# Attention core of a macaron block: probabilities times values in 512-query pieces instead of 256-query chunks

## The reference

```python
x = x + 0.5 * ffn(layernorm(x), ...)          # 8 experts of low rank, top 2
x = x + attn(layernorm(x), wq, wk, wv, wo)    # 16 heads of 128
x = x + 0.5 * ffn(layernorm(x), ...)

# attn
q = rope(einsum('bsd,dnh->bsnh', x, wq)) / sqrt(128)
k = rope(einsum('bsd,dnh->bsnh', x, wk))
v = einsum('bsd,dnh->bsnh', x, wv)
logits = where(causal, einsum('bqnh,bknh->bnqk', q, k), -1e30)
probs = softmax(logits)
attn = einsum('bnqk,bknh->bqnh', probs, v)
return einsum('bqnh,nhd->bqd', attn, wo)
```

## Time and profile before

| what | value |
|---|---|
| median of 3 runs | 1491.52 us (1490.91 to 1491.75) |
| profiled execution, device time | 1489.62 us |
| its span, first to last instruction | 1487.5 us |
| PE matmul / weight load | 1419.2 us (95%) / 1261.8 us (85%) |
| DVE / ACT / POOL busy | 1072.3 / 912.1 / 782.8 us |
| granted TensorE clock, mean | 0.992 |

### The profile page before, as it was taken

One profiled execution on the slowest core, in us unless ns is written; L12 is line 12 of the kernel. 1 busy time (PEld: TensorE's weight loads), 2 busy tenths in 40 slices (PEclk: granted clock), 3 DMA queues, 4 the chain that ended last, 5 costly groups with the idle time before them and its releaser, 6 DMA issues.

```text
span 1487.5 us, 25689 instructions
## 1 busy us (share of the span) xinstructions
PE 1419.2 (95%) x8932; PEld 1261.8 (85%) x8932; DVE 1072.3 (72%) x2395; ACT 912.1 (61%) x1890; POOL 782.8 (53%) x694
## 2 busy tenths in 40 slices
PE   6999999699999999999999999999999988999998
PEld 4778888589998999899989998999899877878886
DVE  7776876777767777777677767776777777775665
ACT  4544444577767767777777667776776654544433
POOL 4655454355555555555555555555555533755443
PEclk9999999899999999999999999999999999999999
DMA  4000001000000000000000000000000020000000
GB/s 167 1 1 1 1 1 50 22 7 23 1 8 15 8 8 8 15 9 8 15 2 8 22 1 8 22 1 8 8 1 1 1 111 1 1 15 1 15 15 15
DMA packets 11422, 23.40 MB, mean 16 GB/s; under 512 B 928, under 2 KB 5024, under 8 KB 11168
## 3 DMA queue, kind: packets, MB, share of 16 engines
q1 hardware_dynamic: 11296, 21.78, 4.4%
HBM read 19.68 MB, written 2.10 MB: 15 GB/s over the span
## 4 chain that ended last, share of the span: by engine, by line
PE 83%; DVE 9%; POOL 3%; issue 3%; ACT 1%; DMA 0%; DVEq 0%; POOLq 0%; ACTq 0%
PE ps L1439 24%; PE ps L1441 24%; PE ps L1440 24%; PE ps L1824 9%; DVE ps L1379 2%; DVE pT_l L327 1%; POOL um_l L327 1%; PE ps L1452 1%; POOL hid_l L327 1%; DVE hid L1079 1%; DVE mixed L1089 1%; POOL w_l L327 0%; POOL mixed_l L327 0%; DVE stats L934 0%; DVE xn L953 0%
## 5 line engine op out<-in xcount | busy, mean ns | idle before, releaser
L624 POOL TENSOR_SCALAR probs<-probs,inv_sum 128x128 f32<-128x128 f32 (+7 forms) x256 | 211.8, 828 | 387.1 <-DVE inv_sum L1314 387.1
L1379 DVE CUSTOM_DVE_ANT_0 ps<-ps,causal 128x128 f32<-128x128 f32 (+7 forms) x256 | 194.7, 761 | 211.0 <-PE ps L1441 209.2
L879 ACT ACTIVATE probs<-ps,neg_max 128x128 f32<-128x128 f32 (+7 forms) x256 | 189.1, 739 | 81.8 <-DVE neg_max L1379 81.8
L327 POOL TENSOR_TENSOR hid_l<-hid,hid_h 128x512 fp32r<-128x512 f32 x80 | 109.5, 1369 | 188.1 <-ACT hid_h L724 188.1
L327 DVE TENSOR_TENSOR pT_l<-ps,pT_h 128x512 fp32r<-128x512 f32 (+3 forms) x384 | 200.4, 549 | 2.8 <-ACT pT_h L858 2.6
L858 ACT ACTIVATE pT_h<-ps 128x512 fp32r<-128x512 f32 (+3 forms) x384 | 174.4, 491 | 34.6 <-PE ps L1824 32.1
L613 POOL TENSOR_TENSOR rot_sin<-swapped,rope 128x512 f32<-128x512 f32 x128 | 165.4, 1292 | 54.7 <-ACT swapped L835 54.7
L1824 PE MATMUL ps<-ident,probs 128*128 128x128 f32 x1152 | 170.9, 275 | 23.1 <-DVE pT_l L327 20.0
L1441 PE MATMUL ps<-pT_h,v_l 128*128 128x256 f32 (+1 forms) x640 | 179.0, 280 | 0.0
L1440 PE MATMUL ps<-pT_l,v_h 128*128 128x256 f32 (+1 forms) x640 | 178.9, 279 | 0.0
L1439 PE MATMUL ps<-pT_h,v_h 128*128 128x256 f32 (+1 forms) x640 | 178.1, 278 | 0.1
(11 more groups left out here) (190 smaller groups left out, 4076.4 us busy)
## 6 DMA issues: line engine op xcount, KB each, us to landing
w_raw<-attn_w SPq DMA_DIRECT2D x32, 256.0 KB, 2.6
w_in<-ffn_w SPq DMA_DIRECT2D x12, 576.0 KB, 8.3
x_sb<-x_in SPq DMA_DIRECT2D x4, 512.0 KB, 5.5
out<-x_sb SPq DMA_DIRECT2D x3, 512.0 KB, 3.2
rope<-rope_w SPq DMA_DIRECT2D x1, 1024.0 KB, 7.7
w_in<-ffn_w SPq DMA_DIRECT2D x2, 264.0 KB, 3.8
expand_raw<-expand_w SPq DMA_DIRECT2D x2, 256.0 KB, 4.8
out<-x_sb SPq DMA_DIRECT2D x2, 256.0 KB, 2.1
```

What stands on the lines that cost most here:

```text
L327: return eng.tensor_tensor(dst, src, high.bitcast(F32), ALU.subtract)
L624: pool.tensor_scalar(probs[s % 4][:, 0:n], probs[s % 4][:, 0:n], inv_sum[:, s % 4:s % 4 + 1], 1.0, ALU.mult, ALU.mult).then_inc(probs_read ...
L879: act.activation(probs[t % 4][:, 0:a * n].rearrange("p (a n) -> p a n", a=a), view, ACT.Exp, bias=neg_max[:, t % 4:t % 4 + 1], scale=-1.0, ...
L1379: dve.tensor_tensor_reduce(out=view, in0=view, in1=causal[:, SEQ - a * n:].rearrange("p (a n) -> p a n", a=a), scale=-SCALE, scalar=HUGE, ...
```

## The change

The diff does the following.

- PV works on 512 queries, half a unit. There are two halves c = 0, 1. Half 0 has key tiles 0 to 3, with 512, 384, 256 and 128 columns. Half 1 has key tiles 0 to 3 with 512 columns each, and key tiles 4 to 7 with 512, 384, 256 and 128. In all, 12 triples per unit in place of 20.
- PV of a unit lies wholly in the steps of the next unit, by the table `PV_AT`: half 0 in step 0, and half 1 in pieces in steps 3, 4, 5 and 6. Step 2 has none.
- The transposed probabilities lie in two tiles: `before` (key tiles 0 to 3 against the queries of half 1) and `own` (the two triangles). `tile_groups` gives the same sizes as before, in another order of key tiles.
- PV results are evicted 512 columns at a time, in steps 1 and 7.
- There is one copy of q. ACT's write of its high part waits until the scores that read the old one are done.
- Values: quarters 0 and 1 of a batch in steps 5 and 7 of the odd unit, quarters 2 and 3 in steps 1 and 7 of the even unit. Output projections: steps 3 and 5 of the even unit and 1 and 3 of the odd one. In the last pair other tables hold, and some layer-norm work of the second feed-forward block moves by one or two steps.
- The order within a step is scores, side work, output projection, PV, transpositions.

```diff
-T_LAG, PV_LAG, OUT_LAG = 2, 5, 8
+T_LAG = 2
-PAIR_SPLITS_AT = {"o": 7, "v": 17, "k": 21, "q": 23}
-DRAIN_STEPS = OUT_LAG + 1
+PAIR_SPLITS_AT = {"o": 13, "v": 25, "k": 21, "q": 23}
+DRAIN_STEPS = 8
+PV_AT = {0: (0, [0, 1, 2, 3]), 3: (1, [0]), 4: (1, [1, 2]), 5: (1, [3, 4]), 6: (1, [5, 6, 7])}
+O_AT = {1: 0, 7: 1}
+DRAIN_PV_AT = {32: (0, [0, 1, 2, 3]), 35: (1, [0, 1, 2, 3, 4, 5, 6, 7])}
+DRAIN_O_AT = {33: 0, 36: 1}
+Y_AT = {3: 0, 5: 1, 9: 2, 11: 3}
+LAST_Y_AT = [{19: 0, 21: 1, 24: 2, 25: 3}, {34: 0, 35: 1, 37: 2, 38: 3}]
-STATS_AT = [20, 21, 23, 24, 35, 37, 39]
-AGGREGATE_AT = [21, 24, 37]
-NORM_AT = [(23, 24), (25, 26), (38, 39)]
+STATS_AT = [20, 22, 25, 26, 35, 36, 39]
+AGGREGATE_AT = [22, 26, 37]
+NORM_AT = [(23, 24), (27, 27), (38, 39)]
 def tile_groups(i):
-    first = 1 - i % 2
-    out = []
-    while first <= i + 1 - i % 2:
-        n = min(4, i + 2 - i % 2 - first)
-        out.append((first, n))
-        first += n
-    return out
+    return [(False, i + 1)] if i < 4 else [(True, 4), (False, i - 3)]
...
+                if i == 1:
+                    q_h = sbuf(st, "q_h", [P, SEQ], F32R)
+                    q_l = sbuf(st, "q_l", [P, SEQ], F32R)
+                    before_l = sbuf(st, "before_l", [P, 4, 512], F32R)
+                k_h.append(sbuf(st, f"k_h{i}", [P, SEQ], F32R))
+                k_l.append(sbuf(st, f"k_l{i}", [P, SEQ], F32R))
...
+        def weighed_row(c, row):
+            if c == 1 and row < 4:
+                return slice(0, 512), (before_h[:, row], before_l[:, row])
+            d = row % 4
+            if c == 0:
+                cols, at = slice(P * d, 512), slice(4 * P * d, 4 * P * d + P * (4 - d))
+            else:
+                cols, at = slice(0, P * (4 - d)), slice(P * (16 - 3 * d), P * (20 - 4 * d))
+            return cols, (own_h[:, at], own_l[:, at])
...
+            if u % 2 == 0 and i in (1, 7):
+                k = 2 + i // 7
+                return "v", u // 2, 4 * (2 * p + u // 2) + k, k
+            if u % 2 == 1 and i in (5, 7) and not (u == UNITS - 1 and last):
+                k = i // 7
                 return "v", (u // 2 + 1) % 2, 4 * (2 * p + u // 2 + 1) + k, k
...
             def rope_high(index, u, k):
                 act.wait_ge(proj_rot, index + 1)
+                if k % 2 == 1 and index >= 4:
+                    act.wait_ge(scores_done, SEQ_TILES * (index // 4 - 1) + 4 * (k // 2) + 4)
...
+            def weigh(q, u, c, rows, first_unit):
+                final = 3 + 4 * c
+                index = 8 * q + 2 * u + c
+                if rows[0] == 0:
+                    need(pe, o_ready, index)
+                if c == 0:
+                    pe.wait_ge(pT_ready, groups_through(q, SEQ_TILES * u + 3))
+                elif rows[0] == 0:
+                    pe.wait_ge(pT_ready, groups_through(q, SEQ_TILES * u + 7) - 1)
+                if c == 1 and 4 in rows:
+                    pe.wait_ge(pT_ready, groups_through(q, SEQ_TILES * u + 7))
...
+                for row in rows:
+                    w = tuple(v[:, b, row, HD * head:HD * head + HD] for v in (v_h, v_l))
+                    cols, probabilities = weighed_row(c, row)
+                    ins = product(ps[:, PV_BANK, cols], w, probabilities, row == 0, row == final, skip=True)
...
-                    chunk = chunk_of_step(p, t, PV_LAG, first)
-                    if chunk:
-                        weigh(*chunk, first and chunk[0] == 0)
-                    y = out_of_step(p, t, OUT_LAG, first)
+                    y = y_of_step(p, t, first, last)
                     if y:
-                        project_out(*y, misc_bank(t))
+                        project_out(*y, y_bank(p, t, last))
+                    work = weigh_of_step(p, t, first)
+                    if work:
+                        weigh(*work, first and t < 2 * SEQ_TILES)
```

More of the change, by code:

```diff
@@ L416, in side_work @@
                 return "v", 0, k, k
-            if u % 2 == 1:
-                if u == UNITS - 1 and last:
-                    return None
+            if u % 2 == 0 and i in (1, 7):
[3 more added lines that the diff above has]
+                k = i // 7
                 return "v", (u // 2 + 1) % 2, 4 * (2 * p + u // 2 + 1) + k, k
@@ L438, in tile_of_step, with unit_before, weigh_of_step, o_of_step @@
             return None if (first and t < lag) or t - lag >= STEPS else (q, s)
-        def chunk_of_step(p, t, lag, first):
-            tile = tile_of_step(p, t, lag, first)
-            if not tile or tile[1] % 2 == 0:
-                return None
-            q, s = tile
-            u, i = unit_of(s)
-            return u, i // 2, 16 * q + 4 * u + i // 2, q, s
-        def out_of_step(p, t, lag, first):
-            chunk = chunk_of_step(p, t, lag, first)
-            if not chunk or chunk[0] % 2 == 0:
-                return None
-            u, c, _, q, _ = chunk
-            return u // 2, c, 4 * (2 * q + u // 2) + c, q
+        def unit_before(p, t, first):
+            if first and t < SEQ_TILES:
+                return None
+            return (p, t // SEQ_TILES - 1) if t >= SEQ_TILES else (p - 1, UNITS - 1)
+        def weigh_of_step(p, t, first):
+            unit = unit_before(p, t, first)
+            work = PV_AT.get(t % SEQ_TILES) if t < STEPS else DRAIN_PV_AT.get(t)
+            return unit + work if unit and work else None
+        def o_of_step(p, t, first):
+            unit = unit_before(p, t, first)
+            c = O_AT.get(t % SEQ_TILES) if t < STEPS else DRAIN_O_AT.get(t)
+            return unit + (c, 8 * unit[0] + 2 * unit[1] + c) if unit and c is not None else None
+        def o_place(u, c, high):
+            if u % 2 == 0:
+                return (oA_h if high else oA_l)[:, 512 * c:512 * c + 512]
+            return (oB_h if high else oB_l)[:]
+        def y_of_step(p, t, first, last):
+            if last:
+                for b in range(BATCH):
+                    if t in LAST_Y_AT[b]:
+                        return p, b, LAST_Y_AT[b][t], 4 * (2 * p + b) + LAST_Y_AT[b][t]
+            if t >= 2 * SEQ_TILES and t - 2 * SEQ_TILES in Y_AT and not last:
+                q, b, c = p, 0, Y_AT[t - 2 * SEQ_TILES]
+            elif t < 2 * SEQ_TILES and t in Y_AT and not first:
+                q, b, c = p - 1, 1, Y_AT[t]
+            else:
+                return None
+            return q, b, c, 4 * (2 * q + b) + c
+        def y_bank(p, t, last):
+            return MISC_BANKS[-1] if last and t >= STEPS - SEQ_TILES else misc_bank(t)
         def score_view(slot, i):
@@ L863, in attention @@
                         rope_high(turn[2], turn[1], turn[3])
-                    chunk = chunk_of_step(p, t, PV_LAG + 1, first)
-                    if chunk:
-                        u, c, index, _, _ = chunk
-                        dst = oA_h[:, 256 * c:256 * c + 256] if u % 2 == 0 else oB_h[:, c % 2]
+                    o = o_of_step(p, t, first)
+                    if o:
+                        _, u, c, index = o
                         act.wait_ge(pv_done, index + 1)
-                        act.activation(dst, ps[:, PV_BANK, 0:256], ACT.Copy).then_inc(o_high, 1)
+                        act.activation(o_place(u, c, True), ps[:, PV_BANK, :], ACT.Copy).then_inc(o_high, 1)
                     side = side_work(p, t, first, last)
@@ L1367, in attention @@
                         need(dve, y_added, index - 3)
-                        dve.tensor_tensor(tiles, ps[:, misc_bank(t - 1), :], tiles, ALU.add).then_inc(y_added, 1)
+                        dve.tensor_tensor(tiles, ps[:, y_bank(p, t - 1, last), :], tiles, ALU.add).then_inc(y_added, 1)
                     turn = rotation_to_end(p, t, first, last)
@@ L1808, in scores @@
                     rows = slice(P * i, P * i + P)
-                    ins = product(dst, (q_h[u % 2][:, rows], q_l[u % 2][:, rows]),
+                    ins = product(dst, (q_h[:, rows], q_l[:, rows]),
                                   (k_h[u % 2][:, keys], k_l[u % 2][:, keys]), True, True)
@@ L1818, in turn @@
                     bank_free(FIRST_PROJECTIONS[3])
-                for n, (slot, count) in enumerate(tile_groups(i)):
+                for n, (is_before, count) in enumerate(tile_groups(i)):
                     need(pe, pT_ready, groups_before(q, s) + n - 1)
@@ L1862, in attention @@
             def attention(p, first, last):
-                if not first:
-                    bank_user.update({1: ("proj", 16 * p), 3: ("v", 8 * p + 1), 7: ("v", 8 * p + 3)})
                 for t in range(STEPS + (DRAIN_STEPS if last else 0)):
```

104 lines of the change are left out of this document (52 added, 52 removed).

## The result

The changed kernel takes 1516.46 us, median of 4 runs (1515.79 to 1517.34), beside 1491.24 us of the kernel before on the same chip: ratio 1.0169, 95% interval 1.0152 to 1.0187. It is 25 us slower; the forecast was 10 us slower, and its range ended at 1511.

What follows compares the result with a forecast made beforehand. TensorE's matmul stream was taken as the bound. Step 2 waits of 15.9 us (even units) and 7.7 (odd), less 13.4 saved in PV, gave +10.2: 1491.5 to 1501.7 us, with 8 in 10 between 1489 and 1511.

Steps and rivals of the forecast that it cites:

- The cover of step 2: PV's 18 matmuls, 2.10 us ahead of step 2's single transposition, hid its wait for DVE; the change removes them.
- the waits 1.06 and 0.55: PE's wait in step 2 for DVE's low part of tile 7, in us: 1.06 in even, 0.55 in odd units.
- The chain of DVE from the values' low part on: Even units, step 2: values' low part, PV's low part (0.60 instead of 0.33), sum, maximum, tile 7's low part, without gap.
- forecast 0.42: PV's matmuls per unit: 6.98 us before, 6.51 after, 0.42 saved with ends 0.36 and 0.48; 13.4 us in 32 units.
- The rival of cheap wide matmuls: PV's 512-column matmuls cost about 131 ns each, gaining 58 us more, 1444 us; chance 0.01.
- Step 7 keeps its wait: PE's transpositions in step 7 still wait 0.8 us for DVE, since no PV stands there before or after.
- Rival 4: A second wait, from q's single copy or bank 7, holds PE in steps 5 to 7: 0.3 us a unit, 1511; chance 0.10.
- the swap has to be done only by the end of step 5's scores: Argument against a second wait: steps 4 and 5 last about 4.0 and 4.3 us, leaving ACT's swap that time.
- Steps 3 and 4 are free of waits: DVE's some 2 us left after step 2 is less than step 3's PE work of some 2.9, so no further wait.
- PE waits in a step other than 2 and 7: One of two signs in the profile after that would show the prediction wrong.
- I take 0, ends -4 and +4: Net effect of the other edits, with the first pair, last unit and steps behind it: 0, between -4 and +4 us.
- two that were priced at nothing: A wait in step 5 and the drain behind the last unit, both counted as 0 us in the sum.

Runs made afterwards that it cites:

- experiment 10: Changed kernel with PV matmuls wider than 256 columns cut to at most 256, output not right: 1528.75 us, 12.3 slower than the changed kernel.
- experiment 2: Changed kernel with POOL's low part of the rotated k or q first in its step: 1504.45 us, 12 faster than the changed kernel.
- Experiment 3: Changed kernel with the last half 1 of PV in two pieces and the expert pick behind the first addition to x: 1510.80 us, 5.7 faster.
- experiment 9: Changed kernel with POOL's low part first, the last half 1 of PV split and the expert pick behind the first addition: 1499.47 us.
- the edit of step 7: DVE's low parts of the turned probabilities ahead of its maximum in step 7: 1506.07 us in the kernel before, 1497.00 in the changed one.
- experiment 1: Changed kernel with DVE's low parts of tile 7 first in step 2: 1527.25 us, 11 slower than the changed kernel.
- experiment 4: Changed kernel with DVE's low parts of tile 7 first in step 2 and, as second edit, POOL's low part first in its step: 1507.97 us.
- experiment 6: Kernel before the change with DVE's low parts ahead of its maximum in step 7: 1506.07 us, ratio 1.0094.

## Why the prediction was right and wrong

- **Direction and main mechanism: right.** The cover of step 2 goes, and the waits 1.06 and 0.55 were measured as 1.07 and 0.53. The chain of DVE from the values' low part on was read rightly from the earlier trace rows.
- **PV: right.** 0.38 by experiment 10, 0.46 by the starts of its matmuls in the two traces (6.97 and 6.51 us a unit), forecast 0.42. The rival of cheap wide matmuls is refuted: 512 columns stay 0.233 us apart.
- **Step 7 keeps its wait: right** (step 7 is 4.36 us long before and after; in the trace after, the transpositions of a step 7 could have started 0.12 behind the matmul at 727.97 and started at 728.96).
- **Rival 4 was turned down by "the swap has to be done only by the end of step 5's scores": this is the step that failed.** The time by which the swap has to be done is right; that it would be done by then doesn't follow from the lengths of PE's steps. The scores of step 5 end at 717.28 and the swap at 717.45. Steps 3 and 4 are free of waits, as forecast, but PE waits in a step other than 2 and 7, which the prediction names as a sign that it is wrong. The rival was named with its place and price (0.3 a unit, 1511) and given 0.10; measured were 0.34 to 0.38 a unit, 10.1 us by the lengths of the steps and 12.0 by the medians of experiment 2. Against it I had set the length of PE's steps 4 and 5 alone and not followed DVE and POOL through step 4 as I did through step 2. The price that was missing is the sum's 1.69 us in place of 0.68. The Trainium skill, page "SBUF — State Buffer", section "SBUF: two separate sides", says that a DVE instruction with two SBUF inputs and a GpSimd instruction that reads SBUF can't run side by side: whoever is first holds the shared port pair to its end. The traces agree: the sum ends at 714.51, 0.55 us behind the end of POOL's low part at 713.96; in experiment 2 it is 619.33, 0.54 behind the end of POOL's scaling at 618.79. The other side shows as well: the scaling that followed the low part at 713.94, while the sum was under way, took 1.03 us and not 0.58. The prediction should have weighed this rule.
- **"I take 0, ends -4 and +4" for the ends: wrong by its size.** The first two units and the last two gained 2.1, but the drain and the block behind it cost 8.5, so the ends cost 6.4. I had looked for the waits of the last unit only the earlier trace rows; two output projections in following steps with one bank between them, and what stands between them on DVE, are in the table of the change. Experiment 3 gave back 5.7.
- With both taken away the kernel stands at 1499.5, 2 us from the forecast (experiment 9). So the terms that were summed were right, and two that were priced at nothing made the rest. That it comes so near is in part luck: 3.0 us of the stretch behind the last scores are still there (268.3 us, before the change 265.3), and runs of one kernel scatter by 1.5 us.

Open stays what the rest of the drain is (1.8 us to the kernel before, experiment 3), and what in the two kernels turns the edit of step 7 from a cost into a gain.

## What to carry to other kernels

When a block of matmuls is moved, list for every step that loses cover or gets other work the chain of all engines that ends in it; one step followed with care and the others by PE's lengths alone missed more than half of the cost. Look there for instructions of two engines that lengthen each other: the profile shows this as a longer instruction, not as idle time. A wait that ends on another engine's order is not always that engine's fault: taking DVE's work forward made PE wait in later steps in three of four trials (experiments 1, 4 and 6), while matmuls put ahead of the waiting instruction took its wait away, with a part coming back in step 5. An edit of the order has no sign of its own; the same one cost 15 us in the kernel before and gained 19.5 in the changed one. And edits of two queues can meet: the second one of experiment 4 gained 12 us alone and made a new wait beside the first.

## What the runs showed of the hardware

- A DVE addition of two SBUF operands (128x512, 0.68 us) took 1.69 beside a POOL subtraction of 1.29 that had begun before it, and 1.00 beside a POOL scaling of 0.58 that had begun before it. Each time it ended 0.54 to 0.55 behind POOL's.
- POOL's subtraction, which was first, kept its 1.29 us. POOL's scaling of 128x384 behind it, which ran into the DVE addition, took 1.02 to 1.04 us in 31 of 32 places of the changed kernel, and 0.58 to 0.60 in all 32 of experiment 2, where it stands ahead of the addition.
- After 3.68 us without a matmul PE ran 0.5 us at the upper level (256 columns some 0.12 apart) and then at 1.2 GHz (0.21 apart) from 1256.33 to 1259.74, where the granted clock is 0.50.
